# Causal masks in 32 by 32 tiles and more fill products in the second attention of a two-layer kernel

## The reference

```python
att = jnp.einsum('bhqd,bhkd->bhqk', q, k) * scale
causal = jnp.tril(jnp.ones((T, T), dtype=bool))      # T = 256
att = jnp.where(causal[None, None], att, jnp.finfo(att.dtype).min)
att = jax.nn.softmax(att, axis=-1)
```

## Time and profile before

| what | value |
|---|---|
| median of 3 executions | 987.14 us (986.79 to 999.11) |
| profiled execution, its own time | 995.33 us |
| span of its trace | 993.3 us |
| mean granted TensorE clock | 0.856 of full |
| busy: PE, DVE, ACT, POOL | 738.5, 646.1, 616.1, 453.9 us |

### The profile page before, as it was taken

One profiled execution on the slowest core, in us unless ns is written; L12 is line 12 of the kernel. 1 busy time (PEld: TensorE's weight loads), 2 busy tenths in 40 slices (PEclk: granted clock), 3 DMA queues, 4 the chain that ended last, 5 costly groups with the idle time before them and its releaser, 6 DMA issues.

```text
span 993.3 us, 21325 instructions
## 1 busy us (share of the span) xinstructions
PE 738.5 (74%) x8182; PEld 573.3 (58%) x8182; DVE 646.1 (65%) x1190; ACT 616.1 (62%) x1139; POOL 453.9 (46%) x484
## 2 busy tenths in 40 slices
PE   6756776989898992466954788687978888888650
PEld 4535555878887892344642445456756766766540
DVE  5765655766666643777567554575677777687647
ACT  5653455766667462675641434475778878878775
POOL 4485763242443454100004665223566666756632
PEclk8777879999999996678885777698999999999985
DMA  9811222011111113400003321300111111110054
GB/s 310 304 45 47 62 64 58 20 50 31 47 47 39 46 42 108 115 1 2 1 1 119 121 85 60 86 13 23 30 39 41 34 39 39 42 36 26 19 158 118
DMA packets 62357, 63.81 MB, mean 64 GB/s; under 512 B 7378, under 2 KB 52322, under 8 KB 62132
## 3 DMA queue, kind: packets, MB, share of 16 engines
q1 hardware_dynamic: 53300, 44.02, 15.1%
q0 software_dynamic: 8960, 18.43, 5.7%
HBM read 31.88 MB, written 30.55 MB: 63 GB/s over the span
## 4 chain that ended last, share of the span: by engine, by line
PE 33%; ACT 19%; DVE 17%; issue 16%; POOL 9%; DMA 2%; another core or an unknown queue 2%; SPq 0%; ACTq 0%; POOLq 0%; DVEq 0%
POOL xs L1877 6%; ACT arena L1220 4%; PE bank L721 4%; ACT L881 3%; PE bank L786 3%; PE bank L675 3%; PE bank L798 2%; PE bank L528 2%; POOL ys L1896 2%; DVE arena L1644 2%; DVE arena L1737 2%; ACT arena L1121 2%; DVE arena L1624 1%; DVE arena L1642 1%
## 5 line engine op out<-in xcount | busy, mean ns | idle before, releaser
L1896 POOL DMA_INDIRECT ys<-arena x152 | 172.3, 1134 | 178.4 <-ACT arena L1149 56.3
L1877 POOL DMA_INDIRECT xs<-arena x128 | 131.3, 1026 | 77.1 <-issue 33.5
L1220 ACT ACTIVATE arena<-bank 128x512 f32<-128x512 f32 x192 | 99.1, 600 | 83.6 <-PE bank L786 62.1
L1737 DVE TENSOR_REDUCE arena<-bank 128x2 bf16<-128x512 f32 (+1 forms) x192 | 119.0, 682 | 41.9 <-PE bank L759 37.8
L661 PE MATMUL bank<-arena 128*128 128x128 bf16 x608 | 105.9, 220 | 6.4 <-DVE arena L1589 3.3
L662 PE MATMUL bank<-arena 128*128 128x128 bf16 x608 | 105.9, 220 | 0.0
L663 PE MATMUL bank<-arena 128*128 128x128 bf16 x608 | 105.9, 220 | 0.0
L881 ACT ACT_TABLE_LOAD x72 | 92.4, 1283 | 1.3
L1725 DVE SCALAR_TENSOR_TENSOR arena<-arena,bank 128x512 bf16<-128x512 bf16 x64 | 46.0, 746 | 71.2 <-ACT arena L1193 68.0
L721 PE MATMUL bank<-arena 128*128 128x256 f32 x256 | 67.2, 410 | 0.9 <-issue 0.9
L661 PEld LDWEIGHTS bank<-arena 128*128 x608 | 60.2, 99 | 9.6 <-issue 6.5
(11 more groups left out here) (236 smaller groups left out, 2063.9 us busy)
## 6 DMA issues: line engine op xcount, KB each, us to landing
xs<-arena SPq DMA_DIRECT2D x19, 516.0 KB, 7.2
arena<-xs SPq DMA_DIRECT2D x38, 258.0 KB
arena<-ys SPq DMA_DIRECT2D x32, 256.0 KB, 5.1
arena<-in_MF SPq DMA_DIRECT2D x8, 512.0 KB
ys<-arena POOLq DMA_INDIRECT x152
arena<-in_x SPq DMA_DIRECT2D x8, 256.0 KB, 5.7
arena<-in_W SPq DMA_DIRECT2D x8, 256.0 KB
xs<-arena POOLq DMA_INDIRECT x128
```

Source lines behind the costliest of these rows:

```text
L1220: act(PT[kt_][:, i, gs[0]:gs[0] + len(gs), :], bank_of["s2", b, n, i][:, :].rearrange("p (g q) -> p g q", q=w), ACT.Exp, scale=8 ** -0.5). ...
L1737: red(negM[b % 2][:, u, 32 * i + gs[0]:32 * i + gs[0] + len(gs)], kv_, op=ALU.max, negate=True).then_inc(m_max.sem, 1)
L1877: eng.indirect_dma_start(xs[l][:, :], bass.IndirectOffsetOnAxis(ap=slot_i[l][:, m:m + 1], axis=0), xrow[:, t, :], None).then_inc(rows_move ...
L1896: eng.indirect_dma_start(ys[l][:, :], bass.IndirectOffsetOnAxis(ap=yid[g % 4][:, j:j + 1], axis=0), y[:, 128 * j:128 * j + 128], None).the ...
```

## The change

Three things. (1) In fifths from 38 on the mask of a bank is added by products of 32 rows by 32 columns: five in s1 (column blocks of 32, 64, 32, 64 and 128), four in s2 (32, 64, 96 and 128), from a new table `masks` of 128 by 256 in bf16; the semaphore is counted up by the last. (2) In the same fifths every round gets as many fills as it has heads a bank (4 or 2), in addition to the three where they were. (3) The table is loaded with layer 1's other small weights, whose semaphore then counts to 96.

```diff
+S1_MASKS = ((96, 96, 192, 32), (64, 64, 192, 64), (0, 0, 96, 32), (0, 64, 128, 64), (32, 0, 64, 128))
+S2_MASKS = ((32, 32, 192, 32), (0, 0, 192, 64), (64, 0, 32, 96), (96, 0, 0, 128))
+FIFTHS_DONE = 38
...
+        masks = sb(256, BF16)
...
-        ld["v"] = ld["proj"] = ld["rw1"] = ld["rb"] = ld["nw"] = sig("ld_layer1", 80)
+        ld["v"] = ld["proj"] = ld["rw1"] = ld["rb"] = ld["nw"] = ld["masks"] = sig("ld_layer1", 96)
...
-            def four_banks(key, until, filled):
+            def fills(fifth, heads):
+
+                return heads * (fifth >= FIFTHS_DONE) + 3 * (fifth in behind_experts)
+
+            def masks_added(k, i, w, w0, parts):
+
+                r = slice(32 * i, 32 * i + 32)
+                kv_ = k[:, :].rearrange("p (n c) -> p n c", c=w)
+                for q, c, m, width in parts:
+                    j = mm(kv_[q:q + 32, :, w0 + c:w0 + c + width], identb[r, r], bc(masks[r, m:m + width], 1, [32, 512 // w, width]),
+                           start=False, stop=False)
+                return j
+
+            def four_banks(key, until, fills):
 
                 four = []
                 for i in range(4):
-                    if i == 3 and filled:
-                        for _ in range(3):
+                    if i == 3:
+                        for _ in range(fills):
                             mm(four[0][1][:, :], identb, selb.rearrange("p g k -> p (g k)"))
                     four.append((i, bank((*key, i), until(i))))
                 return four
...
-                four = four_banks(("s1", b, n), lambda i: m_max.at(b, 4 * n + i), 5 * b + n in behind_experts)
+                four = four_banks(("s1", b, n), lambda i: m_max.at(b, 4 * n + i), fills(5 * b + n, len(gs)))
...
                 for i, k in four:
+                    if 5 * b + n >= FIFTHS_DONE:
+                        masks_added(k, i, w, w - 128, S1_MASKS).then_inc(m_s1.sem, 1)
+                        continue
                     kv_ = k[:, :].rearrange("p (n c) -> p n c", c=w)
                     mm(kv_[:, :, w - 128:w], identb, bc(negb, 1, [128, len(gs), 128]), start=False).then_inc(m_s1.sem, 1)
...
-                four = four_banks(("s2", b, n), lambda i: m_exp.at(b, 4 * n + i), 5 * (b + 1) + n in behind_experts)
+                four = four_banks(("s2", b, n), lambda i: m_exp.at(b, 4 * n + i), fills(5 * (b + 1) + n, len(gs)))
...
                 for i, k in four:
+                    if 5 * (b + 1) + n >= FIFTHS_DONE:
+                        masks_added(k, i, w, 0, S2_MASKS).then_inc(m_s2.sem, 1)
+                        continue
```

More of the change, by code:

```diff
@@ L56, in fifths @@
 def fifths():
-    done, left = 38, 41
+    done, left = FIFTHS_DONE, 41
     for g in range(21):
@@ L1991, in setup @@
                         dma(xs[l][o:o + 1024, :].rearrange("(p r) d -> p (r d)", p=128), zero).then_inc(zeroed[l].sem, 16)
-                for name, o, a in (("v", Wv, "Wv"), ("proj", Wproj, "Wproj"), ("rw1", rw[1], "rw1"), ("rb", rb, "rb"), ("nw", nw, "nw")):
+                for name, o, a in (("v", Wv, "Wv"), ("proj", Wproj, "Wproj"), ("rw1", rw[1], "rw1"), ("rb", rb, "rb"), ("nw", nw, "nw"), ("masks", masks, "masks")):
                     dma(o, A[a]).then_inc(ld[name].sem, 16)
@@ L2110, in _layout @@
     later = token[:, None] < token[None, :]
+    row, col = i[:, None] % 32, i[None, :]
+    rows_masked = np.concatenate([(col < 96) | (col - 96 < row), (col < 64) | (col >= 96) | (col - 64 > row)], axis=1)
+    a["masks"] = c(np.where(rows_masked, -1e30, 0.0).astype(mybir.dt.np(BF16)))
     one = np.ones((128, 1))
```

## The result

| | kernel before | after |
|---|---|---|
| median of 18 executions | 988.46 us | 999.82 us |
| their ends | 984.21 to 999.11 us | 996.11 to 1006.33 us |
| profiled execution, its span | 995.33 us, 993.3 us | 999.41 us, 997.4 us |

The ratio is 1.0119 (95% interval 1.0099 to 1.0140): 1.2% slower, less than the 2% that counts as a difference but well outside its own uncertainty. The rival that is nearest, in its size and partly in its reason, is "TensorE's idle time is used up": 2 us a period, 995 us.

A forecast was written before the change was run, and what follows sets the result against it. No engine was full; a chain of waits hopping between engines bound the kernel. Terms +1.2 + 0.8 + 0.3 - 2.0 = +0.3 us, set on the 987.1 us median, gave 987.4 us, range 979 to 1,000 us.

The forecast's parts named there:

- TensorE's idle time is used up: Rival: added fills leave 3.6 us idle a period, moved waits put fills on the chain; 2 us a period, 995 us; chance 0.22.
- The first bank's mask: First bank's consumer waits for five or four products, not one: +0.07 us (0 to 0.16), some 11 times, +0.8 us in all.
- late handovers go: Rival: fills let semaphores through earlier, three rounds give 0.9 us each, both clock falls go; 982 us; chance 0.20 with clock.
- Fills in unfilled rounds: Two or four fills in s1 and s2 rounds without fills before: hidden by waits or met by shorter masks, cost 0.
- Seven fills: Four-head filled s2: scores 0.78 us later, masks give back 0.42 us, chain +0.36 us; four such rounds, +1.2 us in all.
- Hidden fills: Four-head s1 rounds: four more fills, 0.87 us, fit in waits of 1.41 and 1.70 us; VectorE's slack absorbs later maxima.
- The clock: Low-clock stretches at 662 to 670 and 690 to 697 us: -1.5 us and -0.5 us, together -2.0 us.
- The end: After 952 us the last scatter and join carry the chain, so rounds of fifths 80 to 82 don't move the end.
- Serial masks: Rival: mask products run one after another in all 51 rounds, 2.17 us a four-head set; 1,022 us; chance 0.05.
- Changes of shape: Rival: each array shape change between scores and small masks costs 0.1 us in 51 rounds; +5 us, 992 us; chance 0.07.
- the 25 ns that the prediction set against the change: Opposing rule: matmul starts at least about 25 ns apart, so twenty products need 0.50 us; two-head rounds lose some 0.1 us.

## Why the prediction was wrong

**The first bank's mask.** "+0.07 us, from nothing to 0.16 us. It is on the chain about three times in a period": this step failed. The counting up of five or four products was priced by their starts on TensorE. Measured is 0.54 us for the first count of the s2 at 766 us, and 1.05 us by the last, 1.00 us a period of it on the path. It comes up in one place of the period only; in the filled rounds the consumer is still busy when the count comes, and in s1 the small masks cost nothing (0 us). The trace of before had the warning in it: the 1.33 us of the earlier trace rows, against 0.4 us for the mask. I used it for a rival in which late handovers go. They didn't go (795.55 to 796.93 is 1.38 us), and a new one came.

**Fills in unfilled rounds.** "The s2 behind it ... 0" and "scores some 0.35 us later, masks 0.42 us shorter: 0": failed, 0.75 us a period. In the s2 of 811 us the wait of 0.71 us was to cover 0.43 us carried over from its s1 and 0.87 us of its own. It can't: scores start 16.24 us behind that half's first scores in place of 15.56, +0.68 us. And the shorter masks give nothing back, since ScalarE begins with the first bank, whose count is no earlier: masks to exps takes 1.95 us in place of 1.70 (814.79 to 816.49 before, 812.00 to 813.95 after). The exps are 0.92 us later (18.74 against 17.82 us), and so is the next batch (37.28 against 36.36 us). The saving of a mask set comes at its last bank; it counts only where the next TensorE work is on the path, not where the consumer of the first bank is.

**Seven fills.** "+0.36 us" each, the wait of 0.94 us not given back: right on TensorE, far too high on the path. With large masks at n = 1 the down products behind this round start 17.36 us into the period where they started 16.98 us into it, later by 0.38 us as forecast. But the half is longer by 0.09 us only (35.88 against 35.79 us): by themselves the fills in filled rounds with large masks cost 0.45 us (35.85 to 36.30 us), and small masks give 0.42 us back. What follows takes most of the delay in, which the step left out. So the term of +1.2 us was about 1 us too high, an error to the other side that hid a part of the others. In the change the wait grew to 1.80 us, which is the late count above and not the fills.

**Hidden fills.** Ahead of the four-head s1 rounds the waits of 1.41 and 1.70 us shrank to 0.54 and 0.84 us, by the 0.87 us of four fills: right. VectorE's slack behind the s1 of 764 us was there too: with large masks in s2, n = 1, the fills of fifth 57 start 14.84 us in, though the maxima came 0.43 us later.

**The clock.** Of the -2.0 us the first part came: no fall at 662 to 670 us, 1.00 in place of 0.92, and the batch around it is 1.4 us shorter. The second did not: the low stretch of 689 us is now 680.1 to 690.3 us, 10.2 us in place of 6.8, and began where TensorE had stood idle 4.44 us. Sixteen down products in it took 3.62 us where full clock gives 1.95 to 2.05 us. And I didn't ask the reverse question, whether the clock falls where small masks stand without fills; it does.

**The end.** "the three rounds of fifths 80 to 82 can change without moving the end": failed in that trace. The chain of after, in its last 60 us, goes over TensorE's low clock and the second attention's last rounds, where before it went over the scatters:

```profile
939.14 3.77 PE bank L695 x16
...
946.50 3.58 PE bank L695 x16
...
957.69 1.71 PE bank L758 x4
...
960.62 2.07 ACT arena L1243 x4
```

The stretch takes 2.7 us more. In the single traces of the slower chips it lasts 69.7 to 71.5 us with large masks and nothing beside them in s2 (five kernels, that of before among them) and 72.8 to 77.3 us with small ones (seven, the change among them), which points to the s2 masks there too, by way of count or clock; that was not taken apart, and the 2.7 us stay open.

**The rivals.** Serial masks were refuted by the first masks row (0.45 us, where 2.17 us were forecast). Changes of shape cost nothing that is seen in the period: the period with small masks in all rounds but one is 0.35 us shorter than with large ones. "TensorE's idle time is used up" had 0.22, and its 2 us a period is what was measured on this kind of chip; but half of it is a count, not idle time.

## What to carry to other kernels

Idle time ahead of a product is cover only for what is put there, once; add up what the rounds in front hand on, and look whether the time saved behind comes at the bank that the consumer waits for. Splitting one product into several small ones saves columns, but on some chips the consumer got its count later, and without fills TensorE's clock fell: price both, and the count on the chip, not by the products' starts. Where executions differ by 1% and the effect is 1%, read the period in the trace, and walk from the old kernel to the new one edit by edit at full clock.

## What the runs showed of the hardware

- 32 by 32 products run side by side in both directions: 20 of them, 320 columns a head for four heads in four banks, in 0.45 us, where one after the other needs 2.17 us (an estimate from the 0.217 us of a 512-column product); 16 of one mask set for two heads in 0.33 us. Twenty in 0.34 us leave at most 17 ns from start to start, so the 25 ns that the prediction set against the change don't hold for tiles side by side. By the Trainium skill, TensorEngine Tiling (Array Packing), Key Properties, a change of tiling mode drains TensorE; between a four-head s1's scores and its masks lie 0.33 us with either size (758.34 to 758.67 here, 798.67 to 799.00 in the earlier trace rows), so a smaller tile adds nothing to it in this place.
- A product's count can reach the consumer much later than the product's end as the trace gives it: the first exp starts 0.32 us behind the masks' start in most rounds of two heads, 0.86 us behind sixteen small masks, 1.52 and 2.23 us with tiny products ahead, in the same place of the program. Columns don't explain it; number, shape and place of the products weren't told apart. Two chips of the five on which experiments ran showed no late count in the traced periods.
- These two run the kernel before in 947 and 949 us, the others in 987 to 995 us, with the period at 69.7 us (with the tiny products behind) in place of 72.15 us, at full clock in both. Late counts are part of it. In the second half of the period of before three handovers are late, 1.33, 0.68 and 1.70 us; on the quicker chip they are 0.43, 0.32 and 0.43 us, and the half is 34.35 us in place of 36.36 us. In the first half, which has no late handover that is waited for, it is 35.32 in place of 35.79 us.
- The clock can fall when TensorE's work is thinned out or its waits grow: with the small masks alone it was granted 0.93 and 0.95 of full over whole periods in which the kernel before, with full-array masks, is granted 1.00; with large masks and twelve tiny products in one round 0.98.
